# VectorE's order in a fused transformer kernel: turn(1) and turn(2) placed between a quad's subtraction and its row sums

## What is computed

```python
qkv = shift_tokens(x) @ Wqkv                      # 16 heads of 64
q, k = l2norm(q) * qs, l2norm(k) * ksc
q = q * cos * scale + rotate_half(q) * sin * scale
k = k * cos * inv + rotate_half(k) * sin * inv
sim = einsum(q, k) * 8 + mask                     # windows of 32, each sees 64 keys
x = softmax(sim) @ v @ Wo + x
xn = layernorm(shift_tokens(x)) ; a, gate = split(xn @ W1 + b1)
x = (a * gelu(gate)) @ W2 + b2 + x
```

## Time and profile before

| | |
|---|---|
| median of three executions | 3166.11 us |
| the profiled execution | 3168.24 us |
| its span, first to last instruction | 3166.5 us |
| busy share of the span | PE 95%, DVE 91%, ACT 72%, POOL 57% |
| mean granted TensorE clock | 0.99 of full speed |

### The profile page before, as it was taken

One profiled execution on the slowest core, in us unless ns is written; L12 is line 12 of the kernel. 1 busy time (PEld: TensorE's weight loads), 2 busy tenths in 40 slices (PEclk: granted clock), 3 DMA queues, 4 the chain that ended last, 5 costly groups with the idle time before them and its releaser, 6 DMA issues.

```text
span 3166.5 us, 93664 instructions
## 1 busy us (share of the span) xinstructions
PE 3005.7 (95%) x37896; PEld 1857.5 (59%) x37896; DVE 2880.3 (91%) x2671; ACT 2272.7 (72%) x3707; POOL 1807.9 (57%) x823
## 2 busy tenths in 40 slices
PE   8699999999999999999999999999999999999996
PEld 4356555665665566565566656556656555665653
DVE  5599999999999999999999999999999999999995
ACT  4467777777777777776667777777777777777774
POOL 8556565555656555555445565555656565555652
PEclk9799999999999999999999999999999999999998
DMA  9544544543544544454344354454445445445542
GB/s 317 169 110 116 144 115 107 145 122 98 156 117 101 144 117 117 118 154 113 84 133 106 91 152 117 107 133 124 112 121 141 112 122 133 112 118 134 125 112 59
DMA packets 254405, 398.04 MB, mean 126 GB/s; under 512 B 51148, under 2 KB 84872, under 8 KB 254280
## 3 DMA queue, kind: packets, MB, share of 16 engines
q1 hardware_dynamic: 254280, 396.41, 47.8%
HBM read 64.64 MB, written 19.92 MB: 27 GB/s over the span
## 4 chain that ended last, share of the span: by engine, by line
PE 40%; DVE 23%; ACT 19%; issue 10%; SPq 1%; POOL 1%; DMA 1%; DVEq 0%; ACTq 0%; POOLq 0%
PE ps L848 6%; PE ps L806 5%; PE ps L866 5%; PE ps L882 5%; PE ps L827 5%; PE ps L787 4%; ACT f_ab L1094 4%; DVE f_mx L1362 4%; DVE f_p L1365 3%; ACT f_u L1093 3%; DVE f_p L1377 3%; ACT ps L1105 3%; PE ps L789 3%; PE ps L788 3%; ACT f_p L1111 3%
## 5 line engine op out<-in xcount | busy, mean ns | idle before, releaser
L1291 POOL TENSOR_TENSOR f_w<-f_w,f_ab 128x1024 f32<-128x1024 f32 x192 | 549.2, 2861 | 526.9 <-DVE f_w L1342 526.9
L1296 POOL TENSOR_TENSOR f_ab<-f_w,f_rn 128x1024 f32<-128x1024 f32 x192 | 594.1, 3094 | 390.9 <-DVE f_rn L1352 380.9
L1287 POOL TENSOR_TENSOR f_u<-f_u 128x512 f32<-128x512 f32 x384 | 589.1, 1549 | 365.3 <-ACT f_u L1093 359.8
L1094 ACT ACTIVATE f_ab<-ps,f_pa 128x512 f32<-128x512 f32 x768 | 542.1, 706 | 1.2
L1093 ACT ACTIVATE f_u<-ps 128x512 f32<-128x512 f32 x768 | 467.1, 608 | 99.3 <-PE ps L789 93.6
L1342 DVE TENSOR_TENSOR f_w<-f_ab,f_tan 128x1024 f32<-128x1024 f32 x384 | 500.4, 1343 | 4.1 <-POOL f_ab L1296 2.3
L848 PEld LDWEIGHTS ps<-f_tb,f_v 128*64 128x64 f32 x6144 | 396.0, 137 | 102.1 <-issue 78.5
L848 PE MATMUL ps<-f_tb,f_v 128*64 128x160 f32 (+1 forms) x6144 | 442.2, 297 | 11.9 <-DMA f_tb<-f_pt 10.7
L1105 ACT ACTIVATE ps<-ps 128x512 f32<-128x512 f32 x384 | 204.7, 574 | 340.7 <-PE ps L806 340.2
L787 PE MATMUL ps<-f_xh,f_wh 128*128 128x512 f32 x768 | 380.7, 496 | 54.8 <-ACT f_ab L1094 44.5
L806 PE MATMUL ps<-f_u,f_ones 128*128 128x512 f32 x768 | 370.2, 604 | 6.9 <-POOL f_u L1287 4.1
(11 more groups left out here) (165 smaller groups left out, 4822.9 us busy)
## 6 DMA issues: line engine op xcount, KB each, us to landing
f_kb<-f_ab SPq DMA_DIRECT2D x384, 256.0 KB, 3.6
f_qb<-f_ab SPq DMA_DIRECT2D x384, 256.0 KB, 3.6
f_tb<-f_pt SPq DMA_DIRECT2D x1344, 64.0 KB
f_wh<-split_w SPq DMA_DIRECT2D x48, 384.0 KB, 4.4
f_wl<-split_w SPq DMA_DIRECT2D x48, 384.0 KB, 4.2
a_w_raw<-wqkv SPq DMA_DIRECT2D x24, 384.0 KB, 4.6
split_w<-a_w_hi SPq DMA_DIRECT2D x24, 384.0 KB, 4.6
split_w<-a_w_lo SPq DMA_DIRECT2D x24, 384.0 KB, 5.5
```

The costliest lines, as they stand in the source:

```text
L1094: nc.scalar.activation(ab[:, g % 2, i, :], bank("qk", g, i), ACT.Identity, scale=pa[:, g, i:i + 1]).then_inc(qk_read.sem, 1)
L1287: nc.gpsimd.tensor_tensor(u[:, 2 * i + 1, :], u[:, 2 * i, :], u[:, 2 * i + 1, :], ALU.add).then_inc(sq_sum[i].sem, 1)
L1291: nc.gpsimd.tensor_tensor(w[:, 0:2, :], w[:, 0:2, :], ab[:, k % 2, 0:2, :], ALU.add).then_inc(q_sum.sem, 1)
L1296: nc.gpsimd.tensor_tensor(ab[:, k % 2, 0:2, :], w[:, 0:2, :], rn[:, 0:1, :].broadcast_to([128, 2, N]), ALU.mult).then_inc(rope_q.sem, 1)
```

## The change

Only the order of VectorE's work in a plain step is changed. In such a step turn(1) moves from behind sums(-1) to ahead of it, and turn(2) from behind sums(0), turn_weights(0) and residual() to ahead of all three. Nothing is added or removed; no wait, buffer, or other engine's order is changed. turn(2) moves in step 0 as well.

```diff
                         if prev:
                             less_maximum(-1)
+                        if cur:
+                            turn(1)
+                        if prev:
                             sums(-1)
-                        if cur:
-                            turn(1)
-                        if prev:
                             turn_weights(-1)
                         if cur:
                             add_keys(1)
                             normalise_keys(1)
                             less_maximum(0)
+                            turn(2)
                             sums(0)
                             turn_weights(0)
                         if prev:
                             residual()
                         if cur:
-                            turn(2)
                             add_keys(2)
                         if prev:
                             centred()
```

More of the change, by code:

```diff
@@ L1526, in step @@
                             less_maximum(-1)
-                            sums(-1)
                         if cur:
@@ L1530, in step @@
                         if prev:
+                            sums(-1)
                             turn_weights(-1)
```

## The result

The changed kernel takes 3423.09 us, the median of four executions (3417.08 to 3425.32), against 3165.95 us before in the same set of runs. The ratio is 1.0809, with a 95% interval of 1.0791 to 1.0828. The forecast was 3414 us, in a range of 3340 to 3475.

What follows compares the result with a forecast made beforehand. PE and DVE, both nearly full, were held bound through DVE's residual, which delays ACT, DVE and the next step's PE. 5.1 + 0.8 = 5.9 us over 42 plain steps, 248 us, gave 3416, as median 3414; range 3340 to 3475.

Steps and rivals of the forecast that it cites:

- The circle of three links: Plain step: DVE's less_maximum(2) releases PE's next step, ACT waits for DVE's residual, DVE for ACT; residual's delay passes one for one.
- One reading beside it: Busy times of one plain step of 61.33 us: neither PE nor DVE has 5% to spare.
- 0.2 us a step lost: turn(1) ahead of sums(-1): takes turns with POOL's add_squares(1), most recovered at L1356; bounds -0.15 to +1.1 us.
- the 0.9 us feared: Weights' transfers start up to 1.1 us later, values(-1) may slip from 819.11 to about 820; counted at nothing.
- the residual 5.1 us later: turn(2) ahead of sums(0) waits for POOL's normalise_queries(1): residual at 829.4 instead of 824.30; bounds 4.2 to 5.8 us.
- falls in most steps: PE idles over 4 us ahead of mean, so its clock falls to half: 0.8 us a step, between 0 and 1.7.
- one stretch of 3.4 us at 0.50: PE after its idle time ahead of mean: 3.4 us at half the clock lose up to 1.7 us of work.
- The clock at full: Rival: same wait of turn(2), but PE's clock does not fall; 214 us slower, 3380; chance 0.22.
- turn(2) would not wait as long: Rival: rope_q(1) comes earlier or another engine absorbs delay; residual moves 1.24 us, 3218, up to 3330; chance 0.12.
- it would be faster: Rival: both waits for the exponential go, 2.24 us a step, 94 us in all, 3072; chance 0.06.
- no slack of ACT took up the loss: Rival: no difference, DVE's late work made up behind the residual, needing ACT slack between 824.99 and 834.44; chance 0.03.

Runs made afterwards that it cites:

- The fillers: Changed kernel with 18 matmuls that nobody reads on PE between project(3)'s first half and mean in each plain step: 3382.05 us, ratio 1.0676.
- POOL's other order: add_queries(1) and normalise_queries(1) ahead of add_squares(2): on the changed kernel 3362.57 us, with two buffers w too 3367.16; on the kernel before 3144.42.

## Why the prediction was right

**What bounds the kernel.** The circle of three links held. In the table above only the stretch with the residual and the one behind it have grown by more than 3 us, and the residual's delay reached the next step undiminished. One reading beside it was loose: DVE is idle 3.65 of 61.33 us, which is 6%, not under 5%; nothing hung on it.

**turn(1).** Forecast: 4.4 us for the pair, 0.2 us a step lost. Measured: 4.32 and 4.30 us, and alone 10 us in all (0.29%), which is 0.25 us a step. The size is right, the place only in part: the 0.2 us were to be DVE's lateness at less_maximum(0), and of this 0.04 us came; L1377 of quad 0, behind a POOL that is later itself, takes 0.13 us more. The transfers of quad -1's weights start later, and values(-1) waited 0.25 us in the step shown, less than the 0.9 us feared; nothing came of it, for residual waits for PE twice, 13.5 us in all, as before (12.7).

**turn(2).** Forecast: a start at 822.2, 3.6 us behind the subtraction's end (the text's "idle 3.4 us" beside it was 0.2 us short of its own times), the pair 2.36, L1377 about 2 us, the residual 5.1 us later. Measured: 3.66 us (1079.91 to 1083.57), 2.36, 2.09 and 5.1.

**The clock.** Forecast: falls in most steps, 0.8 us each. Measured: a fall in every plain step, 0.95 us each on average and 40 us in all. The fillers show that it is the clock. The mechanism was right, but that the size came so near was in part luck. The forecast had one stretch of 3.4 us at 0.50 in view. The 8 steps that have just that lose 0.35 to 0.4 us, half of the forecast; the other 34 have 6.8 us at 0.50, which it did not foresee, and lose 0.55 to 1.35 us. Together the term was 6 us too low, which makes most of the 9 us between 3414 and 3423.

**The rivals.** The clock at full would have given 3380, which is what the fillers measured (3382). That turn(2) would not wait as long is refuted by 44 waits. That it would be faster failed where the text put it, at the residual. And no slack of ACT took up the loss.

## What to carry to other kernels

Before moving an instruction into an idle slot, look up when the last reader of its output buffer ends, not only when its inputs are there; the slot here was 1.12 us wide and the buffer came free 3.4 us after it opened. Then follow who waits for what stands behind it: a residual that an idle engine waits for passes each microsecond on to the next step. A long wait of PE can cost a second time through its clock.

An idle time with a clear releaser need not be the one to attack. The gain of 0.65% lay in a duration that was too long, a multiplication of 1.76 instead of 1.22 us whose idle time was zero, because it stood behind GpSimd inside its own duration.

## What was not expected of the hardware

Two instructions of VectorE back to back do not keep SBUF against a waiting GpSimd instruction: GpSimd gets in between them. In the changed kernel's turn(1) they end in turn: GpSimd at 1066.65, VectorE at 1067.73, GpSimd at 1068.88, VectorE at 1069.97. With two of each, VectorE's pair took 4.3 to 4.4 us instead of 2.36 and GpSimd's 3.5 instead of 2.5; where the two of GpSimd were the longer ones, VectorE's pair took 5.53 us. The collision stands in the durations, not in the idle times, so no list of waits shows it, and it moves when either engine is reordered: in three runs (the two with POOL's other order on the changed kernel, and the one on the kernel before) an instruction that had been free before took it over.

Matmuls that nobody reads, 4.06 us of them in each step, bought 0.95 us a step by keeping the granted clock at full.
